# One trip of group statistics, bias loaded as rows, the first image in two halves, another tile order and a third product buffer in a convolution-attention kernel

## The reference

```python
def window_attn(x, Wqkv, bqkv, scale, ws=WS, nh=NH):
    ...
    qkv = (xw @ Wqkv + bqkv).reshape(B, hg * wg, ws * ws, 3, nh, hd)
    q, k, v = jnp.transpose(qkv, (3, 0, 1, 4, 2, 5))
    attn = jax.nn.softmax(jnp.einsum('bgnqd,bgnkd->bgnqk', q, k) * scale, axis=-1)
    o = jnp.einsum('bgnqk,bgnkd->bgnqd', attn, v)
    ...
g = window_attn(xr, Wqkv, bqkv, scale) @ Wproj + bproj
...
l = l.reshape(B, C, H // 2, 2, W // 2, 2).mean(axis=(3, 5))
...
l = window_attn(l, Wqkv, bqkv, scale)
...
l = jax.image.resize(lx + ly, (B, C, H, W), method='bilinear')
...
x = x + _L0_conv_ref(_gn(x), L0_conv_Wqkv, L0_conv_bqkv, L0_conv_Wproj, L0_conv_bproj)
```

## Time and profile before

| | us |
|---|---|
| median of 3 executions | 73.1 (73.03 to 74.18) |
| the profiled execution, its own time | 73.2 |
| its span, first to last instruction | 71.5 |
| outside the span | 1.7 |

### The profile page before, as it was taken

The page is one execution under the profiler, slowest core; times in us unless marked ns, Lnnn a source line. Parts: engine busy times, 40 slices in busy tenths (PEclk is TensorE's granted clock), DMA queues, the critical chain, the costliest instruction groups (busy, mean ns, idle before and its releaser), DMA issues.

```text
span 71.5 us, 1471 instructions
## 1 busy us (share of the span) xinstructions
PE 64.3 (90%) x496; PEld 47.3 (66%) x496; DVE 55.7 (78%) x88; ACT 41.1 (57%) x81; POOL 54.0 (75%) x79
## 2 busy tenths in 40 slices
PE   0997879999999999999999999899999999999900
PEld 0435753665556857757956857599689989998700
DVE  0059899979949998986999999999969985542560
ACT  5200049886688949773874783945839789252200
POOL 5979859855864719999999699999996999980000
PEclk9999999999999999999999999999999999999998
DMA  0998980000000000000000000000000000049565
GB/s 0 307 368 294 332 306 7 0 0 0 9 5 0 0 0 0 0 5 9 0 0 0 5 0 0 0 9 0 0 0 0 0 0 0 0 170 369 216 238 190
DMA packets 2311, 5.07 MB, mean 71 GB/s; under 512 B 768, under 2 KB 1024, under 8 KB 2304
## 3 DMA queue, kind: packets, MB, share of 16 engines
q1 hardware_dynamic: 2160, 4.72, 18.1%
q10 hardware_dynamic: 144, 0.26, 1.0%
HBM read 2.89 MB, written 2.10 MB: 70 GB/s over the span
## 4 chain that ended last, share of the span: by engine, by line
PE 79%; DMA 9%; DVE 2%; issue 2%; SPq 2%; ACT 1%; DVEq 1%; ACTq 0%
PE q_ps L774 12%; PE s_ps L813 10%; PE k_ps L765 9%; DMA x_sb<-in_x 9%; PE v_ps L791 8%; PE ot_ps L827 7%; PE job_ps L850 7%; PE job_ps L867 6%; PE job_ps L742 4%; PE v_ps L788 3%; PE k_ps L850 2%; PE k_ps L867 2%; PE job_ps L754 2%; PE s_ps L850 1%; PE s_ps L867 1%
## 5 line engine op out<-in xcount | busy, mean ns | idle before, releaser
L436 POOL TENSOR_TENSOR pv<-pv 128x512 f32<-128x512 f32 x18 | 22.9, 1275 | 1.0 <-DVE pv L676 0.6
L621 DVE TENSOR_TENSOR qk<-q_sb,k_ps 128x1536 f32<-128x1536 f32 x10 | 17.3, 1734 | 0.7 <-PE k_ps L765 0.4
L676 DVE TENSOR_TENSOR pv<-prob_w,v_ps 128x1536 f32<-128x1536 f32 x9 | 15.6, 1736 | 0.2 <-PE v_ps L791 0.2
L544 ACT COPY ot<-ot_ps 128x512 f32<-128x512 f32 x9 | 5.3, 586 | 7.3 <-PE ot_ps L827 7.3
L578 DVE BATCH_NORM_STATS2 bn<-x_sb 128x6 f32<-128x512 f32 x8 | 5.3, 675 | 4.6 <-DMA x_sb<-in_x 4.6
L765 PE MATMUL k_ps<-xd,w_sb 128*128 128x384 f32 x20 | 8.4, 501 | 0.0
L774 PE MATMUL q_ps<-xt,w_sb 128*128 128x512 f32 x16 | 8.3, 597 | 0.1
L791 PE MATMUL v_ps<-w_sb,xd 128*128 128x128 f32 x60 | 8.3, 275 | 0.0
L507 ACT ACTIVATE q_sb<-q_ps,bias_qkv 128x512 f32<-128x512 f32 x10 | 6.8, 682 | 2.0 <-PE q_ps L774 2.0
L813 PE MATMUL s_ps<-qk,head_sum 128*32 128x192 f32 x160 | 7.5, 329 | 0.0
L791 PEld LDWEIGHTS v_ps<-w_sb,xd 128*128 128x128 f32 x60 | 7.5, 192 | 0.0
(11 more groups left out here) (102 smaller groups left out, 121.0 us busy)
## 6 DMA issues: line engine op xcount, KB each, us to landing
x_sb<-in_x SPq DMA_DIRECT2D x4, 512.0 KB, 5.2
out<-out_sb SPq DMA_DIRECT2D x3, 512.0 KB, 3.3
resize_sb<-in_resize SPq DMA_DIRECT2D x1, 512.0 KB, 5.7
out<-out_sb SPq DMA_DIRECT2D x1, 256.0 KB, 2.0
out<-out_sb ACTq DMA_DIRECT2D x1, 256.0 KB, 2.1
w_sb<-in_L_conv_Wqkv SPq DMA_DIRECT2D x1, 192.0 KB, 4.4
wp_sb<-in_L_conv_Wproj SPq DMA_DIRECT2D x1, 64.0 KB, 5.6
bias_qkv<-in_L_conv_bqkv SPq DMA_DIRECT2D x3, 0.5 KB, 6.0
```

The lines of the kernel that those rows point to most:

```text
L436: nc.gpsimd.tensor_tensor(first, first, other, ALU.add).then_inc(summed[i], 1)
L621: nc.vector.tensor_tensor(qk[:, m % 2, :, :, n % 2, :], q, k, ALU.mult).then_inc(qk_done, 1)
L676: nc.vector.tensor_tensor(to, p, v, ALU.mult).then_inc(pv_done, 1)
```

## The change

The group statistics take one trip to PE instead of two. DVE spreads the raw statistics of each channel (12 numbers of two halves) over four places, of which only the channel's own place in its group is not zero (`in_group`, `bn_apart`). One matmul with a matrix of ones within each group (`group_sum`) then puts the raw statistics of all four channels in each channel's row, and DVE's own aggregation makes mean and variance of them. The bias is loaded as 4 rows of 128 values by two transfers on ACT's queue, turned by PE (`turn_bias`, first in its list, followed by `("zero",)`), and copied out by ACT. Image 0 is loaded in two halves. The two coarse tiles keep their kind, but the first of them is now tile 2 instead of tile 3. The products by values have three buffers. All four lists are written in a new order, the warming matmuls stand at other places, and image 0 is stored last of the first three.

```diff
@@ -32,13 +32,14 @@
...
-TILES = [(0, 0), (0, 1), (1, 0), (None, 0), (1, 1), (2, 0), (None, 1), (2, 1), (3, 0), (3, 1)]
+TILES = [(0, 0), (0, 1), (None, 0), (1, 0), (1, 1), (2, 0), (None, 1), (2, 1), (3, 0), (3, 1)]
...
+PVBUF = 3
...
@@ -91,53 +92,52 @@
...
-        ("mean", 0), ("var", 0), ("mean", 1), ("var", 1), ("xt", 0, 0), ("xt", 0, 1), ("Q", 0), ("zero",), ("K", 0),
...
+        ("bias",), ("zero",), ("gs", 0), ("gs", 1), ("xt", 0, 0), ("xt", 0, 1), ("Q", 0), ("K", 0), ("V", 0),
...
-WARM = {("mean", 0): (4, 2), ("var", 0): (1,), ("mean", 1): (2, 2)}
...
-STORES = [0, 1, 2]
+WARM = {("gs", 0): (4,), ("gs", 1): (4, 2), ("Q", 0): (1,)}
...
+STORES = [1, 2, 0]
...
@@ -163,17 +164,15 @@
...
-        bias_qkv = sb("bias_qkv", [P, 3])
-        bias_p = sb("bias_p", [P, 1])
+        bias_rows = sb("bias_rows", [WIN, P])
+        bias = sb("bias", [P, WIN])
...
-        bn = sb("bn", [P, B, 2, 6])
-        mv = sb("mv", [P, B, 2])
+        bn = sb("bn", [P, B, 12])
+        bn_apart = sb("bn_apart", [P, B, GROUP, 12])
...
-        dev = sb("dev", [P, B])
-        dev2 = sb("dev2", [P, B])
...
@@ -346,13 +347,14 @@
...
-                sp.dma_start(x_sb[:, b, :], x_chan[b]).then_inc(x_loaded[b], 16)
+                if b == 0:
+                    sp.dma_start(x_sb[:, b, 0:512], x_chan[b, :, 0:512]).then_inc(x_half, 16)
+                    sp.dma_start(x_sb[:, b, 512:], x_chan[b, :, 512:]).then_inc(x_loaded[b], 16)
+                else:
+                    sp.dma_start(x_sb[:, b, :], x_chan[b]).then_inc(x_loaded[b], 16)
...
-            for a in range(3):
-                sp.dma_start(bias_qkv[:, a:a + 1],
-                             b_qkv[a * C:(a + 1) * C].rearrange("(p a) -> p a", a=1)).then_inc(bias_loaded, 16)
-            sp.dma_start(bias_p[:, :], b_proj.rearrange("(p a) -> p a", a=1)).then_inc(bp_loaded, 16)
...
@@ -366,14 +368,14 @@
...
-            nc.gpsimd.memset(group_mean[:, :], 1.0 / GROUP).then_inc(consts_set, 1)
+            nc.gpsimd.memset(group_sum[:, :], 1.0).then_inc(consts_set, 1)
...
@@ -393,15 +395,14 @@
...
-                pool.wait_ge(stat_read, 2 * g + 2)
+                pool.wait_ge(mean_turned, g + 1)
...
@@ -409,6 +410,8 @@
...
+                    if b == 0:
+                        pool.wait_ge(x_half, 16)
...
@@ -432,13 +435,13 @@
...
-                first, other = pv[:, n % 2, :, 0, :], pv[:, n % 2, :, i + 1, :]
+                first, other = pv[:, n % PVBUF, :, 0, :], pv[:, n % PVBUF, :, i + 1, :]
...
-                pool.wait_ge(bias_loaded, 48)
-                nc.gpsimd.tensor_tensor(key_bias[:, :], bias_qkv[:, 1:2], bias_qkv[:, 1:2],
+                pool.wait_ge(bias_made, 1)
+                nc.gpsimd.tensor_tensor(key_bias[:, :], bias[:, 1:2], bias[:, 1:2],
...
@@ -471,9 +474,13 @@
...
+            act.dma_start(bias_rows[0:3, :], b_qkv.rearrange("(a p) -> a p", a=3)).then_inc(bias_loaded, 16)
+            act.dma_start(bias_rows[3:4, :], b_proj.rearrange("(a p) -> a p", a=1)).then_inc(bias_loaded, 16)
...
+            act.wait_ge(bias_turned, 1)
+            nc.scalar.copy(bias[:, :], s_ps[:, 0:WIN]).then_inc(bias_made, 1)
...
@@ -573,30 +580,33 @@
         @block.vector
         def _(dve):
+            dve.wait_ge(ident_made, 1)
+            nc.vector.tensor_reduce(in_group[:, :], ident[:, :].rearrange("p (g c) -> p c g", c=GROUP), AX.X,
+                                    ALU.add).then_inc(apart_set, 1)
             def batch_stats(b, half):
-                dve.wait_ge(x_loaded[b], 16)
-                nc.vector.bn_stats(bn[:, b, half, :], x_sb[:, b, half * 512:(half + 1) * 512]).then_inc(bn_done, 1)
+                dve.wait_ge(x_half if (b, half) == (0, 0) else x_loaded[b], 16)
+                nc.vector.bn_stats(bn[:, b, half * 6:(half + 1) * 6],
+                                   x_sb[:, b, half * 512:(half + 1) * 512]).then_inc(bn_done, 1)
                 if half == 1:
                     dve.wait_ge(bn_done, max(nth("DVE", ("bn", b, h)) for h in range(2)))
-                    nc.vector.bn_aggr(mv[:, b, :], bn[:, b, :, :].rearrange("p h s -> p (h s)")).then_inc(mv_done, 1)
-
-            def spread(g):
-                bs, nb = slice(STATS[g][0], STATS[g][-1] + 1), len(STATS[g])
-                dve.wait_ge(mean_summed, g + 1)
-                m = stat_ps[:, 0:2 * nb].rearrange("p (b s) -> p b s", s=2)
-                nc.vector.tensor_tensor(dev[:, bs], mv[:, bs, 0], m[:, :, 0], ALU.subtract).then_inc(dev_done, 1)
-                nc.vector.tensor_scalar(neg_mean[:, bs], m[:, :, 0], -1.0, None, ALU.mult).then_inc(stat_read, 1)
-                nc.vector.tensor_copy(gstat[:, bs, :].rearrange("p b s -> p (b s)"),
-                                      stat_ps[:, 0:2 * nb]).then_inc(stat_read, 1)
-                dve.wait_ge(dev_done, g + 1)
-                nc.vector.tensor_tensor(dev2[:, bs], dev[:, bs], dev[:, bs], ALU.mult).then_inc(dev2_done, 1)
-
-            def variance(g):
-                bs, nb = slice(STATS[g][0], STATS[g][-1] + 1), len(STATS[g])
-                dve.wait_ge(var_summed, g + 1)
-                dve.wait_ge(stat_read, 2 * g + 2)
-                nc.vector.scalar_tensor_tensor(out=gvar[:, bs], in0=stat_ps[:, 0:nb], scalar=EPS, in1=gstat[:, bs, 1],
-                                               op0=ALU.add, op1=ALU.add).then_inc(gvar_done, 1)
+                    dve.wait_ge(apart_set, 1)
+                    nc.vector.tensor_tensor(bn_apart[:, b, :, :], bn[:, b, :].unsqueeze(1).broadcast_to([P, GROUP, 12]),
+                                            in_group[:, :].unsqueeze(2).broadcast_to([P, GROUP, 12]),
+                                            ALU.mult).then_inc(bn_spread, 1)
+            def group_stats(g):
+                before = sum(len(bs) for bs in STATS[:g])
+                dve.wait_ge(bn_shared, g + 1)
+                for i, b in enumerate(STATS[g]):
+                    nc.vector.bn_aggr(gstat[:, b, :], stat_ps[:, i * 48:(i + 1) * 48]).then_inc(gstat_done, 1)
+                bs = slice(STATS[g][0], STATS[g][-1] + 1)
+                dve.wait_ge(gstat_done, before + len(STATS[g]))
+                nc.vector.tensor_scalar(gvar[:, bs], gstat[:, bs, 1], EPS, None, ALU.add).then_inc(gvar_done, 1)
+                nc.vector.tensor_scalar(neg_mean[:, bs], gstat[:, bs, 0], -1.0, None, ALU.mult).then_inc(mean_turned, 1)
             def scale_rows(b, k):
                 g = [b in bs for bs in STATS].index(True)
@@ -665,13 +675,13 @@
...
-                if n >= 2:
-                    dve.wait_ge(ot_made, n - 1)
+                if n >= PVBUF:
+                    dve.wait_ge(ot_made, n - PVBUF + 1)
...
@@ -712,22 +722,24 @@
                 if bank(job) is s_ps:
                     pe.wait_ge(shift_done, BATCHES)
-            def group_means(g):
-
-                bs, nb = slice(STATS[g][0], STATS[g][-1] + 1), len(STATS[g])
-                pe.wait_ge(mv_done, max([j for j in among("DVE", "bn") if j[2] == 1].index(("bn", b, 1)) + 1
-                                        for b in STATS[g]))
+            def share_stats(g):
+                bs = slice(STATS[g][0], STATS[g][-1] + 1)
+                pe.wait_ge(bn_spread, max([j for j in among("DVE", "bn") if j[2] == 1].index(("bn", b, 1)) + 1
+                                          for b in STATS[g]))
                 if g >= 1:
-                    pe.wait_ge(gvar_done, g)
-                nc.tensor.matmul(stat_ps[:, 0:2 * nb], group_mean[:, :], mv[:, bs, :].rearrange("p b s -> p (b s)"),
-                                 start=True, stop=True).then_inc(mean_summed, 1)
-
-            def group_variances(g):
-                bs, nb = slice(STATS[g][0], STATS[g][-1] + 1), len(STATS[g])
-                pe.wait_ge(dev2_done, g + 1)
-                pe.wait_ge(stat_read, 2 * g + 2)
-                nc.tensor.matmul(stat_ps[:, 0:nb], group_mean[:, :], dev2[:, bs], start=True,
-                                 stop=True).then_inc(var_summed, 1)
+                    pe.wait_ge(gstat_done, sum(len(bs) for bs in STATS[:g]))
+                else:
+                    pe.wait_ge(group_made, 1)
+                nc.tensor.matmul(stat_ps[:, 0:48 * len(STATS[g])], group_sum[:, :],
+                                 bn_apart[:, bs, :, :].rearrange("p b c s -> p (b c s)"), start=True,
+                                 stop=True).then_inc(bn_shared, 1)
+            def turn_bias():
+                pe.wait_ge(bias_loaded, 32)
+                nc.tensor.matmul(s_ps[:, 0:WIN], bias_rows[:, :], ident[0:WIN, 0:WIN], is_transpose=True, start=True,
+                                 stop=True).then_inc(bias_turned, 1)
             def turn_tokens(b, k):
                 job = ("xt", b, k)
@@ -781,7 +793,7 @@
...
-                    pe.wait_ge(gvar_done, len(STATS))
+                    pe.wait_ge(gstat_done, B)
...
@@ -877,10 +889,8 @@
...
-                if item == ("mean", 0):
-                    pe.wait_ge(mean_made, 1)
...
```

(2 more changed lines are left out.)

77 lines of the change are left out of this document (38 added, 39 removed), and 42 rows, old and new, of the table ORDER.

## The result

The changed kernel takes 74.31 us (median of 4 executions, 74.03 to 74.38). Executions of the kernel before in the same comparison had a median of 73.64; the ratio is 1.0168, with a 95% interval of 1.0151 to 1.0184. The profiled execution took 74.3 us with a span of 72.5, so 1.8 lie outside it, against 1.7 before. The prediction was 71.6 and the range ended at 73.3: both are missed. Executions of either kernel come 1 to 3 us longer now and then; the ratios leave out those more than 1.5% above the fastest of their kernel, which takes out the upper level of time in e6, e8 and e10, leaves e5 and e9 without a ratio, and sets the profiled execution of e3 aside.

The account below looks back on a forecast made before the run. PE was taken to bound the kernel from Q 0 on, behind the load of x and a little DVE. 73.2 - 0.64 (Q 0) - 0.8 (stretch) - 0.1 (tail) = 71.65, forecast 71.6 us, range 70.8 to 73.3.

Parts of the forecast that it names:

- Spreading: Head, on DVE: spreading the raw statistics over 48 numbers costs 0.2, between 0.15 and the 0.54 of 512.
- rival 2: Head, on PE: the clock rises only behind group 1's matmul, six warming units cost 2.56, total 73.0; chance 13%.
- The bias: Start of PE's list: bias landed at 3.3, hidden until PE's L741 at 3.8; its round trip puts shared statistics at 6.5.
- rival 3: Start of PE's list: the bias lands late and holds up PE, total 73.4 or 75.0; chance 9%.
- Halves: Load of image 0: half comes at most 0.7 earlier; statistics done by 4.35 and by about 5.05 instead of 5.63.
- The scaling: Head, on DVE: first scaling at 8.25 instead of 9.22, second done at 9.85; Q 0 at 10.6, gain 0.64.
- The stretch: PE's almost unbroken work from Q 0 to its end: 55.9 us long instead of 56.7, ending at 66.5.
- The walk: Step-by-step costing of all four lists with durations from the trace: first S at 18.6, PE's end at 66.5.
- Rival 4: Behind Q 0: the wait moves to DVE, V and S wait for it in turn, total 73.0; chance 13%.
- The third buffer: Products by values: keeps P 5 from waiting for O 3, costed at nothing; the e12 forecast said up to 0.3.
- The order: Lists behind the head: part of the 0.8 gained in PE's stretch; loss before the first resize falls from 0.44 to 0.2.
- The tail: Behind PE's end: less is on the way when the last transfer goes out, 0.1 gained.

Follow-up runs that it names:

- e6: Changed kernel with the bias as columns on SP's queue, the zero scores behind Q 0 and image 0 in one transfer: median 72.46 us, ratio 0.9935.
- e8: Changed kernel with the edits of e6 and e7 together: median 72.46 us, ratio 0.9901.
- e10: e9 with the tile order, lists behind the head, two product buffers and stores of the kernel before: median 72.29 us, ratio 0.9859.
- e5: Changed kernel with the two trips of statistics of the kernel before, bias first and halves kept: median 76.94 us, no ratio.
- e9: e8 with the bias as rows again, turned behind the first shared statistics, zero scores behind Q 0: median 73.5 us, no ratio.
- e3: Kernel before with the changed kernel's tile order, lists behind the head, three product buffers and order of stores: ratio 0.9976.
- e7: Changed kernel with the mask in_group in PSUM instead of SBUF: median 72.87 us, ratio 1.0014.
- e13: Changed kernel with POOL's sums of images 0 and 1 moved behind image 1's offset, operands in SBUF: 75.44 us in one execution.
- e1: Changed kernel with one more warming unit on PE between the turned bias and the zero scores: median 73.88 us, ratio 1.0111.
- e12: Changed kernel with two product buffers instead of three: median 76.3 us, ratio 1.0417.
- e2: Changed kernel with image 0 loaded in one transfer: median 73.83 us, ratio 1.0108.
- e14: e9 with one more warming unit ahead of the first shared statistics: median 72.22 us, ratio 0.9898.
- e4: Changed kernel with the tile order, lists from the first product on, two product buffers and stores of the kernel before: median 75.41 us, ratio 1.0304.

## Why the prediction was wrong, by its steps

The step that failed is DVE's way through the head: the scaling at 8.25, Q 0 at 10.6 and the first S at 18.6. Measured were 9.44, 12.38 and 20.94. The first four points below are its parts.

- **Spreading: "0.2".** The unhindered value was right (0.20 and 0.21 in e7 and e13), but I priced it without asking what POOL does meanwhile, and took from the earlier trace rows the two sums of 1.04 "ahead of its power" as harmless, since they don't delay POOL's own work. They delayed DVE: the spreading took 0.54 on average, four times, and the negative mean for two images took 1.00 instead of 0.16, after the change had turned it from a read of PSUM into one of SBUF. S 0 from e1 to e7, where the clock is up in time in both: 20.57 to 19.40, **1.2 us**. Of that the negative mean is 0.67 (e1 to e12) and the spreading 0.50 (e12 to e7, 19.90 to 19.40). The kernel before had the same thing once, at dev's square (0.56 at 6.68, to 7.24, beside POOL's sum until 7.23), where it was covered.

  The Trainium skill, page SBUF — State Buffer, section Who interferes with whom, says that "a DVE instruction with two SBUF inputs contends with a GpSimd instruction that reads SBUF", and that the one that comes later waits for the whole instruction of the other. The rows of the spreading agree, as does e7, where one input is in PSUM. The quoted sentence doesn't cover the negative mean, which has one input. I had not weighed that rule.
- **Clock: "at 2.4 GHz from near 6 us"; rival 2, 13%.** The rival came true. The two matmuls of 512 columns at 5.13 took 2.08 and the six units 2.89, against 1.3 each. Its price of 1.4 on the total was too high, since DVE was late anyway: the changed kernel against e1 gives 0.4. Its own terms (1.28 for the six units, 0.4 for the first two) add up to 1.7, not 1.4. In a good head it costs 1.6 at Q 0 (e9 against e10) and 1.5 in time (e9's two levels), and whether it is paid varies from one execution to the next. "Later gaps did not bring the clock down" was no evidence on when it first rises.
- **The bias: L741 at 3.8, statistics at 6.5.** L741 ran at 3.96, so rival 3 (a late landing) didn't come. The shared statistics came at 7.00, 0.5 late by the clock alone. That it stands in front costs nothing while the halves hold DVE as well, and 1.08 at M 0 together with them (e7 to e9). The prediction's estimate of 3.2 for the landing can't be told from 3.9 here, as PE's turn of the bias starts at 3.96 in every profile with it in front but e2's (4.06).
- **Halves: first "by 4.35", second "by 5.05".** They were done at 4.18 and 5.61. But I costed nothing for what comes behind: image 1 was read 1.1 us later than in e2, at 6.87, past the point where DVE has to be free. It is no chance: DVE or POOL first read image 1 at 6.87 to 7.25 in all eight profiles with halves, and at 5.37 to 5.78 in all eight with image 0 whole. The halves could be read 2.70 and 3.71 after their issues (3.49 - 0.79, 4.92 - 1.21), the whole image 3.30 after its own in e2 (4.09 - 0.79).
- **The scaling 8.25, 9.85; Q 0 10.6.** Measured 9.44, 11.06 and 12.38; without the faults above Q 0 comes at 10.42 (e9, e14), 0.82 before the 11.24 of the kernel before and 0.2 better than I said. What of it is the trip's isn't shown.
- **The stretch, 55.9.** Measured 68.94 - 12.38 = 56.6; 56.3 in e9. The walk from the first S was right to 0.1: 66.5 - 18.6 = 47.9 against 48.00. The 0.1 for K 0 and the coming of S 0 were not: DVE reached M 1 at 19.14. Before the first resize 0.3 was lost, for 0.2 predicted. Rival 4 (waits move to DVE) got it right in one place, 0.60 before S 0, not 1 us.
- **The third buffer at nothing, up to 0.3.** The wrong place and size: not P 5 for O 3 but P 2 for O 0, and 2.8 us behind S 0, 2.0 by the medians (e12). I had asked whether the old order wants the buffer; it is the new one that needs it. The sum isn't touched by it, since the changed kernel has the buffer.
- **The order, part of the 0.8.** Behind S 0 it gives 0.12, in the kernel before's head nothing that can be told (e3), with a good head about 0.1 (e9, e10).
- **The tail, 0.1.** 3.56 before, 3.56 now: nothing.

From the walk's S 0 at 18.6 to 20.94, the profiles give, in this order of edits: 0.16 of the walk itself (e9: 18.76), 0.64 for the bias in front and the halves (e7 to e9), 1.17 for the spreading and the negative mean beside POOL (e1 to e7), 0.37 for the clock (the changed kernel to e1). In the other order the shares differ: e6 alone, with the mask still in SBUF, takes back 1.9 by the medians. So each of these costs is shown, and how they divide the loss isn't. What stays open: why the clock rises in one execution near 6 and in the next not by 9.5, and what the trip alone is worth, as e5 gave no ratio.

## What to carry to other kernels

A small product on DVE with both operands in SBUF cost here its own 0.2 us plus what was left of the POOL operation in progress, each time; some operations with one operand in SBUF were held as well. Look up what POOL does at that time, and put one operand in PSUM if it is busy. Where a change moves a head, find one milestone behind which the rest is constant (here S 0 plus 48.0) and cost everything to that. Price a buffer by the new order, and ask of work put in front of a chain what it does to the clock's rise as well.

## What the hardware showed that I had not expected

- The spreading, with both operands in SBUF, ended 0.06 or 0.07 after the POOL operation that it met, four times of four in the changed kernel. `neg_mean`, with one operand in SBUF, took 1.00 where it started 0.02 after POOL's, and 0.16 in e12, 0.01 after: whether a kernel pays these 0.67 us hangs on hundredths. `gvar`, of the same form, took 0.46 in e4 and 0.36 in e13 and ended 0.03 after POOL's operation. Statistics over 512 columns from SBUF (14.87, 0.68) were not held beside POOL's sum from 14.83.
- The scaling of 128x512 was held too. It took 0.53 at 9.44, where POOL's sum was just over, but 0.81 in e7 to e10 and e14, where it starts beside one, and ended 0.28 or 0.29 after it in all five. The other way round, POOL's `rstd_low` took 0.50 at 9.55 beside the scaling and 0.22 at 12.85. So the best heads here still have up to 0.27 to gain, an estimate from 0.81 - 0.54.
- Two transfers of 256 KB each for image 0 delivered the second half at 4.92 (4.64 to 5.69 in the profiles where DVE waits for it), one of 512 KB all of it at 4.09 in e2.
- Heads with the same instructions on PE and DVE went 1.6 us apart by the rise of PE's clock, which gives such kernels two levels of time, here 72.0 and 73.5.
